# Attention and feed-forward layer on one core: queries and keys in two float32r parts, scores and maxima in row tiles of the TensorE array

## The reference

```
x: (2, 2048, 256) float32; 16 heads of 16
q, k, v = x @ Wq + bq, x @ Wk + bk, x @ Wv + bv        # split in heads
q, k = rope(q), rope(k)                                # interleaved pairs
x = layernorm(x + softmax(q @ k.T / 4) @ v)
xr, xk = mu_r * x + (1 - mu_r) * x_prev, mu_k * x + (1 - mu_k) * x_prev
x = layernorm(x + sigmoid(xr @ W_r.T) * (relu(xk @ W_k.T) ** 2 @ W_v.T))
```

## Time and profile before

| | |
|---|---|
| Median of 3 runs | 1514.62 us (1513.02 to 1515.26) |
| Profiled execution, first to last instruction | 1513.2 us |
| TensorE busy | 1503.6 us, 99% |
| VectorE busy | 1348.9 us, 89% |
| ScalarE busy | 1189.7 us, 79% |
| GpSimd busy | 346.1 us, 23% |
| Opening, to the first scores | about 105 us |
| Heads | 105 to 1430 us |
| Tail | 1430 to 1513 us |

### The profile page before, as it was taken

The page is one execution under the profiler, slowest core; times in us unless marked ns, Lnnn a source line. Parts: engine busy times, 40 slices in busy tenths (PEclk is TensorE's granted clock), DMA queues, the critical chain, the costliest instruction groups (busy, mean ns, idle before and its releaser), DMA issues.

```text
span 1513.2 us, 49334 instructions
## 1 busy us (share of the span) xinstructions
PE 1503.6 (99%) x21940; PEld 1092.1 (72%) x21940; DVE 1348.9 (89%) x1457; ACT 1189.7 (79%) x2177; POOL 346.1 (23%) x348
## 2 busy tenths in 40 slices
PE   9999999999999999999999999999999999999998
PEld 4366777788767787787777877788787667775476
DVE  4669999999999999999999999999999999998596
ACT  3248888888888888888888888888888888888845
POOL 3510322132212212132213221042212000000165
PEclk9999999999999999999999999999999999999999
DMA  6825111131112100121112111111111212000143
GB/s 205 272 82 167 18 23 24 24 79 24 24 24 79 24 12 15 23 79 24 24 24 79 24 24 24 65 17 24 23 23 24 38 24 34 7 3 3 30 99 124
DMA packets 76100, 74.09 MB, mean 49 GB/s; under 512 B 51760, under 2 KB 61360, under 8 KB 74096
## 3 DMA queue, kind: packets, MB, share of 16 engines
q1 hardware_dynamic: 75328, 70.15, 20.4%
q10 hardware_dynamic: 560, 0.79, 0.1%
HBM read 29.50 MB, written 14.16 MB: 29 GB/s over the span
## 4 chain that ended last, share of the span: by engine, by line
PE 99%; ACT 0%; DVE 0%; DMA 0%; issue 0%; POOL 0%; SPq 0%; POOLq 0%; ACTq 0%
PE score_ps L627 29%; PE ring_ps L566 29%; PE pv_ps L585 29%; PE score_ps L540 3%; PE ring_ps L599 2%; PE score_ps L712 2%; PE score_ps L551 1%; PE pv_ps L540 1%; PE score_ps L696 1%; PE pv_ps L696 1%; PE ring_ps L551 0%; PE pv_ps L551 0%; ACT probs L800 0%; PE ring_ps L712 0%; DMA xz<-x_blk 0%; DVE rope L1338 0%
## 5 line engine op out<-in xcount | busy, mean ns | idle before, releaser
L1120 DVE TENSOR_REDUCE tile_max<-ring_ps 128x1 f32<-128x1024 f32 x1024 | 1207.7, 1215 | 115.9 <-PE ring_ps L566 110.3
L800 ACT ACTIVATE probs<-score_ps 128x512 f32<-128x512 f32 x2048 | 1110.3, 598 | 212.6 <-PE score_ps L627 154.0
L627 PE MATMUL score_ps<-q_stack,k_stack 99*32 99x512 bf16 x8192 | 891.0, 380 | 0.9 <-ACT probs L800 0.8
L566 PE MATMUL ring_ps<-k_stack,q_stack 96*32 96x512 bf16 x8192 | 742.7, 379 | 0.0
L585 PE MATMUL pv_ps<-probs,v_aug 128*32 128x512 f32 x4096 | 590.3, 592 | 0.0
L627 PEld LDWEIGHTS score_ps<-q_stack,k_stack 99*32 99x32 bf16 x8192 | 411.3, 95 | 160.3 <-issue 87.3
L566 PEld LDWEIGHTS ring_ps<-k_stack,q_stack 96*32 96x32 bf16 x8192 | 397.7, 97 | 170.4 <-issue 104.1
L585 PEld LDWEIGHTS pv_ps<-probs,v_aug 128*32 128x32 f32 x4096 | 222.4, 111 | 15.7 <-ACT probs L800 0.3
L897 POOL TENSOR_TENSOR neg_cuts<-neg_max,zeros 128x16 bf16<-128x16 f32 x31 | 6.8, 220 | 531.4 <-DVE neg_max L1093 531.4
L889 POOL TENSOR_TENSOR v_aug<-v_all,b_v_s 128x256 f32<-128x256 f32 x32 | 23.4, 732 | 298.1 <-PE pv_ps L585 292.6
L910 POOL TENSOR_TENSOR ctx_part<-ctx_turn,recip 128x256 f32<-128x256 f32 x32 | 19.9, 623 | 234.3 <-DVE recip L1152 234.2
(11 more groups left out here) (105 smaller groups left out, 500.5 us busy)
## 6 DMA issues: line engine op xcount, KB each, us to landing
qk_raw<-probs SPq DMA_DIRECT2D x28, 256.0 KB, 3.8
rope<-qk_raw SPq DMA_DIRECT2D x7, 1024.0 KB, 4.9
rope<-qk_raw SPq DMA_DIRECT2D x14, 512.0 KB, 7.3
q_stack<-rope SPq DMA_DIRECT2D x31, 192.0 KB, 3.7
k_stack<-rope SPq DMA_DIRECT2D x31, 192.0 KB, 4.2
xz<-x_tok SPq DMA_DIRECT2D x2, 2048.0 KB, 11.7
q_stack<-rope SPq DMA_DIRECT2D x31, 128.0 KB, 3.7
k_stack<-rope SPq DMA_DIRECT2D x31, 128.0 KB, 3.7
```

What stands on the lines that cost most here:

```text
L566: mm = pe.matmul(ring_ps[k % 2][g:g + VCOLS, c * TOK:(c + 1) * TOK], q_stack[0:ROWS, buf, qt * P + g:qt * P + g + VCOLS], k_stack[0:ROWS, ...
L627: mm = pe.matmul(score_ps[n % SCORE_BANKS][g:g + VCOLS, :], k_stack[0:ROWS_M, h % STACKS, kt * P + g:kt * P + g + VCOLS], queries[:, j], s ...
L800: act.activation(probs[:, kt % 2, j, :], score_ps[n % SCORE_BANKS][:, :], ACT.Exp, scale=SCALE).then_inc(exps_done, 1)
L1120: dve.reduce_max(tile_max[:, h % 2, unit // 2, unit % 2:unit % 2 + 1], slot[:, :], AX.X)\
```

## The change

Queries and keys are cut into two parts of type float32r (4 bytes a value) instead of three of bf16: 3 bands, 48 rows, and two rows for the maximum, 50 in all. Stacks lie in pairs: even heads on partitions 0 to 63, odd heads on 64 to 127 (`stack_rows`). A score block and a half unit of maxima are one instruction each, 128 columns wide on those rows. `period` issues one product of maxima after j = 0 and one after j = 1, and the gate products of the last head right behind the values.

```diff
-PARTS = 3
+PARTS = 2
+SIDES = 2
+SIDE_ROWS = P // SIDES
-QUAD_STEPS = 6
+QUAD_STEPS = 4
-NEG_LOADS = 2
+NEG_LOADS = 1
-        q_stack = sb("q_stack", [P, STACKS, SEQ], BF16)
-        k_stack = sb("k_stack", [P, STACKS, SEQ], BF16)
+        q_stack = sb("q_stack", [P, STACKS // SIDES, SEQ], F32R)
+        k_stack = sb("k_stack", [P, STACKS // SIDES, SEQ], F32R)
+        def stack_rows(h, first, count):
+            side = h % SIDES * SIDE_ROWS
+            return slice(side + first, side + first + count)
+        def slot_of(h):
+            return h // SIDES % (STACKS // SIDES)
...
+            sp.wait_ge(ones_set, 1)
...
                 for c in range(2):
-                    for g in range(0, P, VCOLS):
-                        mm = pe.matmul(ring_ps[k % 2][g:g + VCOLS, c * TOK:(c + 1) * TOK],
-                                       q_stack[0:ROWS, buf, qt * P + g:qt * P + g + VCOLS],
-                                       k_stack[0:ROWS, buf, lo + c * TOK:lo + (c + 1) * TOK], start=True, stop=True)
+                    mm = pe.matmul(ring_ps[k % 2][:, c * TOK:(c + 1) * TOK], q_stack[rows, slot, qt * P:(qt + 1) * P],
+                                   k_stack[rows, slot, lo + c * TOK:lo + (c + 1) * TOK], start=True, stop=True)
...
-                        for g in range(0, P, VCOLS):
-                            mm = pe.matmul(score_ps[n % SCORE_BANKS][g:g + VCOLS, :],
-                                           k_stack[0:ROWS_M, h % STACKS, kt * P + g:kt * P + g + VCOLS],
-                                           queries[:, j],
-                                           start=True, stop=True)
+                        mm = pe.matmul(score_ps[n % SCORE_BANKS][:, :], k_stack[rows, slot, kt * P:(kt + 1) * P],
+                                       queries[:, j], start=True, stop=True)
                         mm.then_inc(scores_ready, 1)
-                        if j == 1:
-                            for _ in range(2):
-                                next(work, None)
+                        if j < 2:
+                            next(work, None)
                         if j == BLOCKS - 2:
                             pv_before(h, kt)
-                        if (h, kt, j) == (LAST, 1, 0):
-                            pe.wait_ge(ring_freed, RING_CREDIT + RING_TOTAL)
-                            next(first_r)
+                            if h == LAST and kt > 0:
+                                if kt == 1:
+                                    pe.wait_ge(ring_freed, RING_CREDIT + RING_TOTAL)
+                                    next(first_r)
+                                next(first_r, None)
                     for _ in work:
                         pass
-                    if h == LAST and kt > 0:
-                        next(first_r, None)
```

More of the change, by code:

```diff
@@ L9 @@
 F32 = mybir.dt.float32
+F32R = mybir.dt.float32r
 BF16 = mybir.dt.bfloat16
@@ L154, in build @@
     turned_d = nc.dram_tensor("y_turned_late", (A_GROUPS, CHUNKS * P, TOK), F32, kind="Internal").ap()
-    neg_d = nc.dram_tensor("neg_turned_rows", (2, P, NEG_LOADS, VCOLS), BF16, kind="Internal").ap()
+    neg_d = nc.dram_tensor("neg_turned_rows", (2, P, VCOLS), F32, kind="Internal").ap()
     with ExitStack() as ctx:
@@ L205, in build @@
         warm = stage[:, STAGES - 1, :].bitcast(BF16)[:, 0:TOK]
[L207 to L210, removed]
+        cuts = rope[:, 0:4 * SEQ].rearrange("p (b a t) -> p b a t", b=2, a=PARTS)
+        raw = rope[:, 4 * SEQ:5 * SEQ]
+        swapped = rope[:, 5 * SEQ:6 * SEQ]
+        tables_s = rope[:, 6 * SEQ:8 * SEQ].rearrange("p (n w t) -> p n w t", n=BLOCKS, w=2)
         taken = [0]
@@ L230, in build @@
         relu = free[:, 6 * TPB * DIM:7 * TPB * DIM].rearrange("p (c t) -> p c t", c=CHUNKS)
[L232 to L235, removed]
+        y_second = probs[:, :, :, :].rearrange("p g j t -> p (g j t)").rearrange("p (b t d) -> p b t d", b=BLOCKS, t=TPB)
         y_blk = [y_half[:, n] for y_half in (y_first, y_second) for n in range(BLOCKS)]
@@ L362, in load_part @@
             def load_part(h, part, t, sides="qk", signal=None):
-                buf, side, row = h % STACKS, h // QUAD % 2, h % QUAD * HEAD_DIM
+                buf, slot, side, row = h % STACKS, slot_of(h), h // QUAD % 2, h % QUAD * HEAD_DIM
                 q = cuts[row:row + HEAD_DIM, side, :, t]
@@ L368, in load_part @@
                 for a, reps in BAND_GROUPS:
-                    rows = slice(first * HEAD_DIM, (first + reps) * HEAD_DIM)
+                    rows = stack_rows(h, first * HEAD_DIM, reps * HEAD_DIM)
                     first += reps
                     if a == part and "q" in sides:
-                        sp.dma_start(q_stack[rows, buf, t], q[:, a:a + 1, :].broadcast_to([HEAD_DIM, reps, t.stop - t.start]))\
+                        sp.dma_start(q_stack[rows, slot, t].bitcast(F32), q[:, a:a + 1, :].broadcast_to([HEAD_DIM, reps, t.stop - t.start]))\
                             .then_inc(signal or stack_in[buf], DMA)
@@ L375, in load_part @@
                     if reps - 1 == part and "k" in sides:
-                        sp.dma_start(k_stack[rows, buf, t], k[:, 0:reps, :]).then_inc(stack_in[buf], DMA)
+                        sp.dma_start(k_stack[rows, slot, t].bitcast(F32), k[:, 0:reps, :]).then_inc(stack_in[buf], DMA)
                         yield
@@ L409, in load_neg @@
                 sp.wait_ge(neg_out, (h + 1) * DMA)
[L410 to L414, removed]
+                dst = q_stack[stack_rows(h, ROWS, PARTS), slot_of(h), :].bitcast(F32)
+                sp.dma_start(dst.rearrange("a (t i q) -> a t i q", i=P // VCOLS, q=VCOLS),
+                             neg_d[h % 2].rearrange("(i a t) q -> a t i q", i=P // VCOLS, a=PARTS))\
+                    .then_inc(neg_in[h % STACKS], DMA)
             sp.dma_start(w_qk_s[:, :, 0:P], w_first).then_inc(w_first_in, DMA)
@@ L559, in maximum @@
                 buf, qt, lo = h % STACKS, unit // 2, unit % 2 * 2 * TOK
+                rows, slot = stack_rows(h, 0, ROWS), slot_of(h)
                 if unit == 0:
@@ L620, in period @@
                         n = item(h, kt, j)
-                        queries = q_stack[0:ROWS_M, h % STACKS, :].rearrange("r (c j t) -> r j c t", j=BLOCKS, t=VCOLS)
+                        rows, slot = stack_rows(h, 0, ROWS_M), slot_of(h)
+                        queries = q_stack[rows, slot, :].rearrange("r (c j t) -> r j c t", j=BLOCKS, t=VCOLS)
                         if n < SCORE_BANKS:
@@ L766, in cut_high @@
                 act.wait_ge(rot_ready, n + 1)
[L767 to L772, removed]
+                act.activation(cuts[:, 0, 0, t].bitcast(F32R), raw[:, t], ACT.Copy).then_inc(high_ready, 1)
             take(BLOCKS)
@@ L872, in _ @@
         def _(pool):
-            pool.memset(k_stack[ROWS:ROWS_M, :, :], 1.0).then_inc(ones_set, 1)
+            pool.memset(k_stack[VCOLS:SIDE_ROWS, :, :].bitcast(F32), 1.0)
+            pool.memset(k_stack[SIDE_ROWS + VCOLS:P, :, :].bitcast(F32), 1.0).then_inc(ones_set, 1)
             pool.wait_ge(ones_set, 1)
@@ L896, in cut_maxima @@
                 after(pool, neg_flipped, h)
[L897 to L900, removed]
-                pool.tensor_tensor(neg_cuts[:, 1, :], neg_rest[:, :], zeros[:, :], ALU.add).then_inc(neg_step, 1)
-                pool.wait_ge(neg_step, h * 3 + 3)
-                pool.tensor_tensor(neg_cuts[:, 2, :], neg_rest[:, :], neg_cuts[:, 1, :], ALU.subtract)\
+                pool.tensor_tensor(neg_cuts[:, 0, :].bitcast(F32R), neg_max[:, :], zeros[:, :], ALU.add).then_inc(neg_step, 1)
+                pool.wait_ge(neg_step, h + 1)
+                pool.tensor_tensor(neg_cuts[:, 1, :].bitcast(F32R), neg_max[:, :], neg_cuts[:, 0, :], ALU.subtract)\
                     .then_inc(neg_cut, 1)
@@ L970, in _ @@
                 t = block_of(n)
-                pool.wait_ge(mid_ready, n + 1)
-                pool.tensor_tensor(cuts[:, 0, 2, t], raw[:, t], cuts[:, 0, 1, t], ALU.subtract).then_inc(first_lows, 1)
+                pool.wait_ge(high_ready, n + 1)
+                pool.tensor_tensor(cuts[:, 0, 1, t].bitcast(F32R), raw[:, t], cuts[:, 0, 0, t], ALU.subtract)\
+                    .then_inc(first_lows, 1)
             pool.wait_ge(b_v_in, DMA)
```

64 lines of the change are left out of this document (18 added, 46 removed).

## The result

The changed kernel takes 1596.4 us (median of 4 runs, 1595.5 to 1597.0) against 1514.5: a ratio of 1.0544 (95% interval 1.0529 to 1.0559). It is slower by 82 us; the forecast was 57 us slower. The profiled execution spans 1593.6 us, 80.4 more than before.

The account below looks back on a forecast made before the run. TensorE's order of work was taken as the bound, with VectorE and ScalarE within 12%. Heads 0 to 29 +32.1, head 30 +1.4, last head +13.3 and opening +10.2 gave +57.0 on 1514.6: 1572 us, range 1450 to 1635.

Parts of the forecast that it names:

- Price of the changes of tiling: TensorE, between scores and values: two changes cost 0.32 us a cycle together, bounds 0 and 0.62.
- My split into 0.20 and 0.12: 0.20 us from the values' 32-column tiling to wide products, 0.12 us back to 32 columns.
- the opening: 32 projections alternating with maxima, each with a change of tiling in and out at 0.32 us: +10.2 us.
- Exposed weights of scores 2: Scores 2 waits for its bank, so its 128-column weight load is not ahead: 0.08 us more, bounds 0 and 0.19.
- Overlapped cycles: 12 of a head's 16 cycles, maxima and scores on different row halves: 2.58 us each.
- The product's slot: One float32r score or maximum product takes 0.217 us, like the bf16 group; upper bound 0.86.
- same-row: Cycles 12 to 15 of a head, scores and maxima on the same row half, no overlap: 2.92 us each.
- heads 0 to 29: 12 cycles at 2.58 and 4 at 2.92 us make 42.64 against 41.57 a head: +32.1 us in all.
- Last two heads: Head 30 +1.4 us; last head +13.3 us, its gate products entering the loop at 0.43 us a cycle.
- No overlap: Row halves don't stream together, every cycle with maxima takes 2.92 us: 1699 us; chance 0.06.
- Half rate: Float32r products take slots of 0.43 us: about +440 us, 1955 us; chance 0.04.
- A cheap change of tiling: Changing the tiling costs 0.10 us a cycle or less, VectorE bounds overlapped cycles: 1452 us, floor 1438; chance 0.34.

Follow-up runs that it names:

- e1: Kernel before, still bf16 in three parts on common rows, with scores and maxima as single 128-column products instead of four 32-column ones: 1646.3 us, ratio 1.0878.
- e2: Changed kernel with the values as one float32 product of 64 rows by 128 columns a cycle, most of their sum left out: 2010 to 2067 us.
- e8: Changed kernel with its two parts, and the maxima's, in bf16 instead of float32r: 1493.9 us, ratio 0.9863 to the kernel before.
- e5: Changed kernel with the last head's gate products moved back between scores 3 and scores 0: 1594.1 us, ratio 1.0526 to the kernel before.
- e4: Changed kernel with heads 0 and 1 of each four on the lower row half, 2 and 3 on the upper: 1635.9 us, ratio 1.0810.
- e9: Changed kernel with the two parts in bf16 and the maxima 6 units ahead instead of 8: 1478.7 us, ratio 0.9766 to the kernel before.
- e3: Changed kernel with the maxima 4 units ahead instead of 8: 1604.4 us, ratio 1.0607 to the kernel before.
- e6: Changed kernel with the values as one float32 product of 128 rows by 128 columns a cycle, three of four blocks left out: 1626.3 us, ratio 1.0744.

## Why the prediction was right, and where its sum was short

*Direction and mechanism held.* The change was expected to be paid for by two changes of tiling in each cycle, inside the loop from scores 3 over the exponential and scores 2 to the values. That loop is in the trace, as the wait ahead of scores 2 and as cycles of 2.61 us without any maxima. e1 puts the changes of tiling into the kernel before, and head 0 of e2 takes them out of the changed one.

*Price of the changes of tiling: right as a sum.* Taken 0.32 us, from one example in the tail. Measured in the float32r kernel: 0.09 into the values, 0.14 out of them, and 0.10 to 0.11 for weights that are not ahead (the first wide product lasts 0.50 instead of 0.39), 0.33 to 0.34. My split into 0.20 and 0.12 was off; 0.24 of it is there with either type, the rest only with float32r. In the opening it was +10.2 forecast and 10.6 measured.

*Exposed weights of scores 2: 0.08 taken, 0.11 measured.* Overlapped cycles 2.61 instead of 2.58.

*The product's slot: the term that was mis-sized.* I took 0.217 us for a float32r product, from the bf16 groups. On the same rows such products stand 0.237 apart (8 x 0.02 = 0.16 a cycle): 3.08 us instead of 2.92. e1 and e8 show that it is the type and not the width, since wide bf16 products keep 0.217. In part this was made up for by luck: I counted four cycles of a head as same-row in full, and the first of them took 2.70. Together heads 0 to 29 lose 53.9 us instead of 32.1, and this 21.8 is nearly all of the 23.4 that the span exceeds the sum. Why a float32r product on the same rows takes 0.24 was not taken apart; its weight load of 0.18 to 0.19 us is the obvious suspect, as the bf16 one of 0.10 doesn't do it.

*Last two heads: +14.7 forecast, 15.8 measured.* The gate products do enter the loop: 3.05 us a cycle against 3.01. e5 shows that their old place would have cost nearly the same in changes of tiling, 2.90 us a cycle.

*The rivals.* No overlap: refuted by the common starts at 701.54 and by e4. Half rate: refuted, slots are 0.24. A cheap change of tiling: refuted by e1. Its world can be read in head 0 of e2, cycles of 2.31 us. That run shows a mechanism that I had not among the rivals, the fall of the clock; whether it would have come in a kernel that multiplies all the values isn't shown.

## What to carry to other kernels

Before a product is halved by running two side by side, follow the dependent chain that it lies in (here bank, exponential, bank) and put each change of the array's tiling there: with float32r they cost 0.34 us a pair, and with the slower weights of scores 2 that was all that the overlap gave (2.61 us a cycle against 2.60); with bf16 they cost 0.24, and 0.2 was left (2.39). Two parts of the cheaper type, overlapped in row halves, were worth 1.4%, and 2.3% with one same-row cycle fewer, where float32r cost 5.4%, so try the type and the tiling separately. The bf16 pair holds fewer digits, and no run has it on common rows, so what the row halves alone are worth to it wasn't measured. And when work is moved ahead of or behind its use by fewer cycles, reckon the small DMA chain at its end: 4 units were too few, 6 enough.

## What was not expected of the hardware

The granted clock fell to its lower level, 1.2 GHz, in e2, where TensorE was busy in 90 to 95% of the stretches shown; it dropped between 220 and 230 us and the page shows it at about half for all of the heads that follow. e9, busy 95% of its span, kept 0.999, with four 32-column value products on all 128 rows where e2 had one on 64. So busy time in the records doesn't tell whether the clock will hold; which difference decides was not tested. Apart from e2, the four runs of e3 read 0.989 to 0.995 and one of e6 0.993; all others were at 0.998 or above.
